# A two-layer decoder kernel: start-up in finer steps, GpSimd taking root epsilons and time-step products, routing by taking out

## What is computed

```
# layer 0
hidden, gate = split(x @ W_in)                       # 2 x 512 channels
hidden = silu(causal_conv(hidden, 4 taps) + bias)
dt, Bm, Cm = split(hidden @ W_x)                     # 128, 16, 16
dts = softplus(dt @ W_dt + b_dt)
for l: state = exp(dts*A)*state + dts*Bm*hidden;  y[l] = sum_n state[n]*Cm[l, n]    # 16 states a channel
x = norm(x + ((y + hidden*D) * silu(gate)) @ W_out)
x = norm(x + softmax(norm(att) * gamma + beta))      # att from x and a product of the context with itself
scores = softmax(x @ Wr); w = scores, kept at the best 2 of 8 experts, else 0
x = norm(x + sum_e w[e] * expert_e(x) + shared(x))
# layer 1
x = norm(x + gated linear recurrence(x))             # its own root mean square inside
x = norm(x + mix with an adjacency from the context, 76 largest of 256 a row)
x = norm(x + best 2 of 8 experts + shared)
```

## Time and profile before

| | us |
|---|---|
| median of three runs | 667.3 (667.09 to 668.12) |
| the profiled execution, its own time | 664.68 |
| its span in the trace | 662.9 |
| mean granted clock of TensorE | 0.902 of full speed |

### The profile page before, as it was taken

The page is one execution under the profiler, slowest core; times in us unless marked ns, Lnnn a source line. Parts: engine busy times, 40 slices in busy tenths (PEclk is TensorE's granted clock), DMA queues, the critical chain, the costliest instruction groups (busy, mean ns, idle before and its releaser), DMA issues.

```text
span 662.9 us, 8987 instructions
## 1 busy us (share of the span) xinstructions
PE 543.9 (82%) x2504; PEld 390.2 (59%) x2504; DVE 525.3 (79%) x1261; ACT 427.4 (64%) x955; POOL 227.0 (34%) x333
## 2 busy tenths in 40 slices
PE   4938564689877965899779998998899999999957
PEld 3526353457755643577557766767577668677634
DVE  0248988897889998999899979999999896664342
ACT  2468753798976973994999688969994632262211
POOL 1023654524552554355254424644440101101000
PEclk9778657689959996899889999999999999999969
DMA  7194010256006601472006703620470233224000
GB/s 220 40 382 157 0 65 0 57 137 225 0 1 194 197 13 63 123 214 66 1 0 176 234 1 95 190 61 1 136 210 2 66 117 102 62 67 141 0 9 8
DMA packets 29297, 63.56 MB, mean 96 GB/s; under 512 B 4864, under 2 KB 8192, under 8 KB 28736
## 3 DMA queue, kind: packets, MB, share of 16 engines
q1 hardware_dynamic: 29248, 62.98, 30.9%
HBM read 61.85 MB, written 1.11 MB: 95 GB/s over the span
## 4 chain that ended last, share of the span: by engine, by line
PE 44%; DVE 34%; issue 13%; ACT 6%; DMA 1%; POOL 0%; DVEq 0%; SPq 0%; POOLq 0%; ACTq 0%
PE work L552 25%; PE work L603 8%; DVE acc L1118 6%; DVE st L1102 6%; PE h_bank L528 5%; PE work L528 4%; DVE m L1053 3%; DVE wk L1057 2%; DVE h_tok L1012 2%; DVE du L1029 2%; DVE bst L940 2%; ACT dA L888 2%; DVE row L948 1%; DMA skip<-in_skip 1%; DVE mv L941 1%
## 5 line engine op out<-in xcount | busy, mean ns | idle before, releaser
L498 POOL TENSOR_TENSOR dbu<-du,b_rows 128x512 f32<-128x512 f32 x128 | 162.6, 1271 | 125.5 <-DVE st L1102 95.0
L888 ACT ACTIVATE dA<-dts,a_neg 128x127 f32<-128x127 f32 x512 | 156.8, 355 | 29.9 <-DVE st L1102 28.9
L1102 DVE TENSOR_TENSOR_SCAN st<-dA,dbu 128x512 f32<-128x512 f32 x128 | 155.7, 1217 | 14.9 <-ACT dA L888 13.1
L528 PE MATMUL h_bank<-ident,st 128*128 128x128 f32 x512 | 90.2, 310 | 40.4 <-DVE st L1102 40.2
L552 PE MATMUL work<-stream,xsT 128*128 128x352 f32 x320 | 112.4, 491 | 5.5 <-DVE h_tok L1012 3.3
L528 PEld LDWEIGHTS h_bank<-ident,st 128*128 128x128 f32 x512 | 69.0, 160 | 71.6 <-DVE st L1102 57.8
L1118 DVE SCALAR_TENSOR_TENSOR acc<-h_bank,c_cols,acc 128x512 f32<-128x512 f32 x128 | 93.7, 732 | 14.2 <-PE h_bank L528 9.7
L552 PEld LDWEIGHTS work<-stream,xsT 128*128 128x128 f32 x320 | 60.2, 202 | 35.6 <-DVE h_tok L1012 5.7
L521 POOL TENSOR_TENSOR rstd<-var,mhalf 128x1 f32<-128x1 f32 x32 | 18.3, 572 | 121.8 <-DVE var L942 93.8
L764 ACT ACT_TABLE_LOAD x44 | 56.5, 1283 | 3.2 <-PE work L552 2.5
L1012 DVE SCALAR_TENSOR_TENSOR h_tok<-h_tok,wf,work 128x176 f32<-128x176 f32 (+2 forms) x136 | 43.6, 374 | 15.7 <-PE work L552 15.6
(11 more groups left out here) (155 smaller groups left out, 846.2 us busy)
## 6 DMA issues: line engine op xcount, KB each, us to landing
stream<-in_stream SPq DMA_DIRECT2D x80, 352.0 KB, 3.7
stream<-in_stream SPq DMA_DIRECT2D x32, 384.0 KB, 3.6
b_rows<-b_dram SPq DMA_DIRECT2D x32, 256.0 KB, 4.9
stream<-in_stream SPq DMA_DIRECT2D x8, 256.0 KB, 2.8
wg<-in_wg SPq DMA_DIRECT2D x1, 1280.0 KB, 8.0
wu<-in_wu SPq DMA_DIRECT2D x1, 1280.0 KB, 10.6
wd<-in_wd SPq DMA_DIRECT2D x1, 1280.0 KB, 13.3
xT<-in_xT SPq DMA_DIRECT2D x4, 256.0 KB, 4.0
```

The costliest lines, as they stand in the source:

```text
L498: gp.tensor_tensor(tile, du[:, batch % 2, :, lo:hi], b_rows[:, b % 2, k:k + 1, :].to_broadcast([P, ET, P]), ALU.mult).then_inc(s["dbu_read ...
L528: return nc.tensor.transpose(dst, src, ident[:, :])
L888: last = A(dA[i % DA_RING][:, t, 1:P], dts[:, batch % 2, t, lo + 1:hi], ACT.Exp, scale=a_neg[:, t, k:k + 1])
L1102: V.tensor_tensor_scan(st[:, i % ST_RING].rearrange("p t l -> p (t l)"), dA[i % DA_RING].rearrange("p t l -> p (t l)"), dbu[:, i % DBU_RIN ...
```

## The change

1. **Finer start.** Stage `pre` has 7 steps: `hid0` and `hid1` are steps of their own, `dt` is projected ahead of `bT`, and the ln, `dts` and `du` are made for each half of 128 columns (k = 5, 6), with semaphores that count halves. `a_neg` and the clearing of `dA` are moved into k = 2.
2. **Loads in order of need.** Six parts: part 0 has `xT` of batch 0, the first half of `w_in` (512 KB), `cw` and `cb`; then the tables of `pre`; then `ident`, `skip` and `xT` of batch 1; then the second half of `w_in` and the context. A first ScalarE instruction on a constant brings the silu table in while the loads run.
3. **GpSimd** adds epsilon itself (56 small instructions, ahead of its power), makes `dts` and `du` for batches 1 to 3 (12 instructions of 128 x 512; VectorE keeps batch 0's, four of them), and `a_first` in one instruction of 128 x 64 for each batch, after the first state of the unit instead of ahead of it.
4. **Experts by taking out** (layer 0): the two best scores are struck out of a copy of the scores and the copy is subtracted from them, in three instructions where five stood.
5. **New order strings and banks** for all engines.

```
-        w_in = load("w_in", [P, HT, 2 * E], d["w_in"], 0)
+        w_in = sb("w_in", [P, HT, 2 * E])
+        loads.append((w_in[:, :, 0:E], d["w_in"][:, :, 0:E], 0))
...
+        ident = load("ident", [P, P], d["ident"], 2)
+        skip = load("skip", [P, ET], d["skip"], 2)
+        loads.append((w_in[:, :, E:2 * E], d["w_in"][:, :, E:2 * E], 3))
...
+            def root_of(layer, variance, eps):
+                if eps:
+                    links[0] += 1
+                    gp.tensor_scalar(var[layer][:, :], variance, eps, None, ALU.add).then_inc(s["pool_link"], 1)
+                    pool.wait_ge(s["pool_link"], links[0])
+                    variance = var[layer][:, :]
+                gp.tensor_tensor(rstd[layer][:, :], variance, mhalf[:, :], ALU.pow).then_inc(rstd_ready[layer], 1)
...
+            for stage, b, k in pool_order:
+                if stage == "pre" and k >= 5 and b:
+                    u, p = LT * b + k - 5, b % 2
+                    lo, hi = (k - 5) * P, (k - 4) * P
+                    pool.wait_ge(s["sp_ready"], u + 1)
+                    gp.tensor_tensor(dts[:, p, :, lo:hi], dts[:, p, :, lo:hi], za[:, :, lo:hi], ALU.add)\
+                        .then_inc(s["dts_ready"], 1)
+                    pool.wait_ge(s["dts_ready"], u + 1)
+                    gp.tensor_tensor(du[:, p, :, lo:hi], dts[:, p, :, lo:hi], hs[:, p, :, lo:hi], ALU.mult)\
+                        .then_inc(s["du_ready"], 1)
...
+                    if hands_on(b) and k == 1:
+                        pool.wait_ge(s["dts_ready"], LT * (batch + 1))
+                        gp.tensor_tensor(a_first[:, :, :], a_neg[:, :, :].rearrange("p t n -> p n t"),
+                                         dts[:, batch % 2, :, hi:hi + 1].rearrange("p t l -> p l t").to_broadcast([P, N, ET]), ALU.mult).then_inc(s["keep_exp"], 1)
...
+            act.wait_ge(s["ones_ready"], 1)
+            A(es[:, :], ones[:, :], ACT.Silu)
...
             def stats(src, layer=0):
                 link(V.bn_stats(bst[layer][:, :], src))
-                link(V.bn_aggr(mv[layer][:, :], bst[layer][:, :]))
-                V.tensor_scalar(var[layer][:, :], mv[layer][:, 1:2], eps, None, ALU.add).then_inc(var_ready[layer], 1)
+                V.bn_aggr(mv[layer][:, :], bst[layer][:, :]).then_inc(var_ready[layer], 1)
...
-                    link(V.max_index(out=i8[lay][:, :], in_max=t8[lay][:, :], in_values=sc[:, :]))
-                    route(0, t8[0])
+                    link(V.tensor_copy(top2[:, 0:2], t8[lay][:, 0:2]))
+                    link(V.match_replace(out=rest[:, :], in_to_replace=top2[:, :], in_values=sc[:, :], imm_value=0.0))
+                    link(V.tensor_tensor(wf[lay][:, 0:8], sc[:, :], rest[:, :], ALU.subtract))
...
     "pool": [
-        "ppppppppppppppppppppsaaaaaaaaaaaaaaaaaaaaaaaaaaaaaaaaaaaaaaaaaaaaaaaaaaaaaaaaaaaa0000ssssssss1111sssssssssssss",
+        "ppppppppppppsaaaaaaaaaaaaaaaaaaaaaaaaaaaaaaaaaaaaaaaaaaaaaaaaaaaaaaaaaaaa0000ssssssssssssss1111sssssssssss000s",
```

More of the change, by code:

```diff
@@ L216, in decoder @@
[L216 to L220 removed]
+            loads.append((xT[:, b], d["xT"][:, :, b * L:(b + 1) * L], 5))
+        wqT = load("wqT", [C, C], d["wqT"], 3)
+        wkT = load("wkT", [C, C], d["wkT"], 3)
+        wkvT = load("wkvT", [C, C], d["wkvT"], 3)
+        b_k = load("b_k", [C, 1], d["b_k"], 3)
@@ new lines, in decoder @@
+        gam = load("gam", [P, 1], d["gam"].partition_broadcast(P), 3)
+        w_out = load("w_out", [P, ET, H], d["w_out"], 4)
+        x_rows = sb("x_rows", [P, 2, H])
+        loads.append((x_rows[:, :, :], d["x"][:, 0:2, :], 4))
+        lng = load("lng", [P, L], d["lng"].partition_broadcast(P), 4)
+        lnb = load("lnb", [P, L], d["lnb"].partition_broadcast(P), 4)
+        iota = load("iota", [P, F0.experts], d["iota"].partition_broadcast(P), 4)
+        wr = load("wr", [P, HT, F0.experts], d["wr"], 4)
@@ L553, in product, with in_projection @@
                 return last
-            def in_projection(b, names, first):
-                for i, n in enumerate(names):
-                    t = claim(n, b)
-                    for f in range(2):
-                        m = first + (2 * i + f) * P
-                        last = product(t, f * L, lambda c: w_in[:, c, m:m + P], lambda c: xT[:, b % 3, c, :], HT, L)
-                    fill(last, n, b)
+            def in_projection(b, n, first):
+                t = claim(n, b)
+                for f in range(2):
+                    m = (first + f) * P
+                    last = product(t, f * L, lambda c: w_in[:, c, m:m + P], lambda c: xT[:, b % 3, c, :], HT, L)
+                fill(last, n, b)
             def streamed(k, u):
@@ new lines, in _ @@
+                    for tap in range(KC - 2, -1, -1):
+                        off = KC - 1 - tap
+                        for f in range(2):
+                            t = 2 * k + f
+                            if tap < KC - 2:
+                                dve.wait_ge(s["dve_link"], kept_tap[f])
+                            last = V.scalar_tensor_tensor(
+                                out=du[:, p, t, off:L], in0=work_bank(f"hid{k}", b)[:, f * L:(f + 1) * L - off],
+                                scalar=cw[:, t, tap:tap + 1], in1=du[:, p, t, off:L], op0=ALU.mult, op1=ALU.add)
+                            if tap:
+                                kept_tap[f] = mark(last)
@@ new lines, in _ @@
+                    release(last, f"hid{k}", b)
+                if stage == "pre" and k == 2 and b == 0:
+                    for t in dA:
+                        last = V.memset(t[:, :, 0:1], 0.0)
+                    last.then_inc(s["dA_cleared"], 1)
+                    dve.wait_ge(s["a_exp"], 1)
+                    V.tensor_scalar(a_neg[:, :, :], a_neg[:, :, :], -1.0, None, ALU.mult)\
+                        .then_inc(s["a_ready"], 1)
+                if stage == "pre" and k >= 5 and b == 0:
+                    u, p = LT * b + k - 5, b % 2
+                    lo, hi = (k - 5) * P, (k - 4) * P
+                    dve.wait_ge(s["sp_ready"], u + 1)
+                    V.tensor_tensor(dts[:, p, :, lo:hi], dts[:, p, :, lo:hi], za[:, :, lo:hi], ALU.add)\
+                        .then_inc(s["dts_ready"], 1)
+                    dve.wait_ge(s["dts_ready"], u + 1)
+                    V.tensor_tensor(du[:, p, :, lo:hi], dts[:, p, :, lo:hi], hs[:, p, :, lo:hi], ALU.mult)\
+                        .then_inc(s["du_ready"], 1)
```

268 lines of the change are left out of this document (115 added, 153 removed).

## The result

| | before | after |
|---|---|---|
| median, us | 667.2 (666.8 to 668.1, 4 runs) | 645.5 (644.7 to 647.5, 4 runs) |
| the profiled execution, its own time | 664.68 | 645.74 |
| its span in the trace | 662.9 | 644.0 |
| ratio after to before | | 0.968 (0.965 to 0.970) |

What follows compares the result with a forecast made beforehand. VectorE was taken to pace the kernel up to unit 3, both engines nearly full to unit 7, then TensorE's chain. 282 + 329 + 29.5 + 1 + 1.5 = 643 us of span, plus 4.4, gave 647 us (640 to 656, chance 0.60).

Steps and rivals of the forecast that it cites:

- What bounds the kernel: Whole kernel: VectorE paces it up to unit 3; only time won ahead of unit 3 reaches the end in full.
- Loads: At the start: half of `w_in` lands at about 6 (5.3 to 7.5), the convolution begins 4.6 us sooner.
- `gam` and `hs`: At the start: TensorE waits for `gam` and goes on at about 14; `hs` begins at about 18.5, 2 us sooner.
- VectorE at the start: Ahead of the first scan: rounds fill VectorE's wait, busy 25, idle about 21, first scan at about 46 (44 to 50).
- Work taken from VectorE: Epsilons, `dts` and `du`, `a_first` and routing: together 25 us less on VectorE, no gain by itself.
- Unit 3: Its gate multiply comes at 282 instead of 298.3: VectorE busy 239 + 2, idle 21 + 20.5.
- Behind unit 3: From unit 3's gate multiply to the end: TensorE's work 329 as before, its idle time 29.5 instead of 35.4.
- GpSimd's answer becomes the wait: Rival: VectorE waits at the 56 roots and at `dbu` behind six pairs; about 670, slower; chance 0.09.
- Side by side: VectorE beside GpSimd: 12 new GpSimd instructions may hold up VectorE's, 0 to 7.7 us; 1.5 charged.
- Only the start counts: Rival: VectorE's lighter load buys nothing, part of the start's 18 us is lost again; 656 to 661; chance 0.14.
- The whole gain: Rival: VectorE's 25 us come through too, idle times of 8.0 and 12.4 fall to 5; 631 to 638; chance 0.12.
- no change: Rival: the idle time won at the start comes back whole at unit 3; 667; chance 0.05.

Runs made afterwards that it cites:

- e7: Changed kernel with two clears of a scratch tile added on VectorE to each of 32 states of units 1 and 2, ahead of unit 3: 664.4 us.
- e8: Changed kernel with the same 64 VectorE clears in the states of units 5 and 6 instead: 661.0 us.
- e1: Changed kernel with the 56 epsilon additions alone put back on VectorE: 647.1 us.
- e6: Changed kernel with the second half of `w_in`, the context and five small tables (`gam` last) loaded ahead of the projections' tables: 641.5 us.
- e3: Changed kernel with the first adjacency's ten rounds and mask put between the first five scans, not in VectorE's idle start: 657.0 us.
- e2: Changed kernel with `dts` and `du` of batches 1 to 3 alone put back on VectorE: 646.3 us.
- e4: Changed kernel with epsilons, `dts` and `du`, `a_first` and routing all undone; steps, loads and order strings of the change stay: 656.8 us.
- e10: e6 with a tighter start: `sim` evacuated ahead of `acc`, `kv` and gate, batch 0's `cT` and `gram` made behind `z`: 640.0 us.

## Why the prediction was right, and where only its sum was

647 was forecast, 645.5 measured. Point by point:

- **What bounds the kernel.** That VectorE paces it up to unit 3 holds: the moment of unit 3 is its busy plus its idle time in each kernel, and e7's load passed on nearly whole. That "only time won ahead of unit 3 passes on to the end in full" is the step that failed: e8 shows four fifths or more for time between units 3 and 6. (That 12.0 of the 18.9 us were won behind unit 3 is no such proof: 5.2 of them are TensorE's work that moved or shrank, and 6 of the 6.8 us of idle time were forecast there.) It was argued from TensorE's idle time (12.4 us of 188.7), as if an engine with little idle time covered the others. Behind unit 6 it does hold: the epsilons count for nothing there (e1).
- **Loads.** Forecast about 6, at most 7.5; the last transfer of part 0, `cb` with 2 KB, landed at 7.9, 5.2 us after its issue, as long as 1024 KB took before. Halving `w_in` did bring its own landing forward, from 6.7 to 5.3, within the forecast; but `cb` was then the gate, and it landed later than before (7.9, 7.1). In the thirteen traces with the change `cb` took 4.3 to 5.4 us. The forecast priced the large transfer and left the small one behind it at nothing. The convolution began 2.7 us sooner, not 4.6.
- **`gam` and `hs`.** The wait was named but set at 14; it ended at 16.0, since `gam` took 5.1 us and not the 3.0 of the earlier trace rows. With the half clock behind it `hs` came at 21.8, not 18.5: later than before. In e1, where `gam` landed just as late (15.9) but the clock stayed full, `hs` came at 20.0, so the clock is some 1.7 of it. e6 shows the price of both, 4.0 us at the end by the medians.
- **VectorE at the start.** Busy 25.4 (forecast 25), idle 24.1 (21), first scan 49.5 (46, within 44 to 50). That the rounds fill the idle time is the core of the forecast, and e3 puts 11.5 us on it.
- **Work taken from VectorE.** 25 us forecast, 17.9 in the page's busy time. Routing saves 3.3 us by its groups instead of 5, since the subtraction takes 0.307 and the copy 0.286 us on average, with one meeting with a long GpSimd instruction in each (both 0.17 in e2); `dts` and `du` save 7.2 instead of 8.4, since one `du` met a `dbu` and took 1.64; and instructions that were not changed got longer by some 3 us, one of layer 1's scans among them (1.52 us in place of 0.4), because they met a long GpSimd instruction. What it is worth (e4: 11.3) had been booked as no gain by itself: too low.
- **Unit 3.** Forecast 282 = 241 + 41.5; measured 291.4 = 247.1 + 44.3. VectorE's sum in the new order was 6 us short, and TensorE has 959 matmuls ahead of unit 3 where it had 927 (217.3 us and 214.7), which the forecast of equal sums missed.
- **Behind unit 3.** Forecast 329 + 29.5 + 2.5 = 361; measured 352.6 = 324.0 + 28.6. TensorE's idle time was right to a microsecond. Its busy time was 5 lower: some 30 matmuls had moved ahead of unit 3, and its total came out 2.6 lower at the same granted clock of 0.902. The two misses of 9.4 and 8.4 us are opposite in sign, and that is why the sum stands: the span of 643 (measured 644.0) is right by luck in these two terms. The step from span to median, 4.4 us, was too large as well: 1.7 held, the 2.6 by which the median before had lain above the profiled execution did not come again (645.5 and 645.7).
- **GpSimd.** 255.8 (255); the addition 0.233 us (0.2); `a_first` 0.52 (0.4). Waits for `rstd` at L987 10.9 us in all, a little above the forecast's "some 10"; before, the same instruction waited 5.2 for layer 1's root and 1.2 for layer 0's. They don't lead VectorE's waits (19.9 us are for TensorE at L992). The rival in which GpSimd's answer becomes the wait did not come: all of the 10.9 us lie behind unit 6, where they lengthen nothing (e1).
- **Side by side.** Charged 1.5 us, too little: instructions of VectorE that were lengthened beside one of GpSimd's of 128x512 cost 15.2 us in all before and 18.7 in the changed kernel, 3.5 more, each counted against the short ones of its group (16.7 to 20.5 in the experiments, so that some of it is which instructions happen to meet). One of them is the changed kernel's `du`, which paid 0.95 (1.64 less 0.69). Put back on VectorE (e2), `dts` took 0.895 us on average against 0.69 alone: 1.2 us for six. The Trainium skill, "SBUF — State Buffer", section "Who interferes with whom", says that such two-input VectorE instructions contend with GpSimd's reads; these rows agree. The Trainium skill, "Perfetto Trace Analysis", section "Optimizing Scalar/DVE Operations", says that moving work between these two might not help; the end can't tell that from a gain here (0.8 us, e2), but to unit 3 the move brought 3.9 us.
- **The rivals.** *Only the start counts* falls: e4 has the start and the order, and is 11.3 us worse. *The whole gain* (631 to 638) did not come; e10 comes near it (640.0) by a tighter start, which is not that rival's mechanism. *GpSimd's answer becomes the wait* (670) and *no change* (667) fall with the result and the waits above.

Left open: why TensorE's granted clock between units 5 and 6 was 0.96 in the changed kernel and 0.94 in e10, 1.7 us of its busy time there (78.78 and 80.48), for the same matmuls.

## What to carry to other kernels

Idle time of the pacing engine before its main loop is the cheapest place for work that is due later: having ten rounds there was worth some 10 us. When a transfer gates such a start, order the queue by first need down to the last 0.5 KB table: in these first 16 us a small transfer took as long as a large one, and the new order gave 4.0 us by the medians. Price handed-over work by where it stands before asking what the receiver adds: the epsilon additions returned a fifth of their length over the whole kernel, but about half ahead of unit 6, where VectorE is nearly full, and nothing behind it, where VectorE rests half of the time. `a_first` and the routing together returned 60% to 90%; whether that is because nobody awaits them at once, or because more of them stands ahead of unit 6, was not separated.
